# A token shift of 127 partition rows, issued as one transfer or as two of 112 and 15 rows

## The reference

```python
def shift_tokens(t):
    a, s = jnp.split(t, 2, -1)
    s = jnp.pad(s, ((0, 0), (1, 0), (0, 0)))[:, :-1]
    return jnp.concatenate([a, s], -1)

def ffn_layer(x, g, bln, W1, b1, W2, b2):
    mu = x.mean(-1, keepdims=True)
    var = ((x - mu) ** 2).mean(-1, keepdims=True)
    xn = (x - mu) / jnp.sqrt(var + 1e-05) * g + bln
    hg = xn @ W1 + b1
    a, gate = jnp.split(hg, 2, -1)
    return a * jax.nn.gelu(gate, approximate=False) @ W2 + b2

for i in range(DEPTH):                       # 6
    x = attn_layer(shift_tokens(x), Wqkv[i], q_scale[i], k_scale[i], Wo[i]) + x
    x = ffn_layer(shift_tokens(x), ln_g[i], ln_b[i], W1[i], b1[i], W2[i], b2[i]) + x
```

## Time and profile before

| | before |
|---|---|
| median of 3 runs | 1936.04 us |
| the three runs | 1918.3, 1936.04, 7699.03 us |
| the profiled execution's own time | 1925.6 us |
| its span, first to last instruction | 1923.8 us |
| mean granted TensorE clock, share of full speed | 0.928 |

### The profile page before, as it was taken

The page is one execution under the profiler, slowest core; times in us unless marked ns, Lnnn a source line. Parts: engine busy times, 40 slices in busy tenths (PEclk is TensorE's granted clock), DMA queues, the critical chain, the costliest instruction groups (busy, mean ns, idle before and its releaser), DMA issues.

```text
span 1923.8 us, 67850 instructions
## 1 busy us (share of the span) xinstructions
PE 1577.6 (82%) x28560; PEld 1265.7 (66%) x28656; DVE 1382.6 (72%) x2564; ACT 1251.0 (65%) x4601; POOL 1263.7 (66%) x1492
## 2 busy tenths in 40 slices
PE   7588978888879789879789888797898787987974
PEld 5366766766767567667567676676676676766753
DVE  4686876876867778678868777786687686776752
ACT  3376766767757667667667676586676675775761
POOL 2487666776766767667758667676677586776640
PEclk8698989989989999999999899998898998999997
DMA  3011111012111011111111211111211101111110
GB/s 108 13 35 57 39 50 40 26 52 60 35 40 40 27 52 48 43 51 32 40 49 34 60 39 44 30 37 40 60 37 52 41 24 41 42 37 30 36 29 28
DMA packets 50157, 80.61 MB, mean 42 GB/s; under 512 B 8227, under 2 KB 16086, under 8 KB 49854
## 3 DMA queue, kind: packets, MB, share of 16 engines
q1 hardware_dynamic: 49854, 76.27, 14.1%
HBM read 18.62 MB, written 1.05 MB: 10 GB/s over the span
## 4 chain that ended last, share of the span: by engine, by line
PE 46%; DMA 18%; DVE 15%; POOL 9%; ACT 8%; issue 5%; SPq 0%; DVEq 0%; POOLq 0%
DMA xsh<-xr 17%; PE ps L393 6%; PE ps L439 5%; PE ps L449 5%; PE ps L386 5%; ACT pr L647 4%; PE ps L480 4%; PE ps L409 3%; PE ps L388 3%; PE ps L387 3%; DVE t L946 3%; DVE t L948 3%; POOL t L795 3%; PE ps L420 2%; ACT sq L610 2%
## 5 line engine op out<-in xcount | busy, mean ns | idle before, releaser
L776 POOL TENSOR_TENSOR t<-t 128x512 f32<-128x512 f32 x384 | 486.9, 1280 | 86.6 <-DVE t L948 85.4
L647 ACT ACTIVATE pr<-ps,nmax 128x64 f32<-128x64 f32 x1536 | 460.1, 344 | 0.9 <-DVE nmax L963 0.9
L795 POOL TENSOR_TENSOR t<-t,rn 128x512 f32<-128x512 f32 x384 | 397.2, 1056 | 7.5
L393 PE MATMUL ps<-consts,t 128*128 128x128 f32 x1536 | 245.3, 295 | 148.3 <-POOL t L795 138.4
L647 ACT ACTIVATION_READ_ACCUMULATOR pr<-ps,nmax 128x1 f32 x1536 | 364.5, 238 | 0.0
L946 DVE TENSOR_TENSOR t<-ps,rope 128x512 f32<-128x512 f32 x384 | 262.9, 685 | 106.1 <-PE ps L393 74.5
L393 PEld LDWEIGHTS ps<-consts,t 128*128 128x128 f32 x1536 | 192.3, 151 | 204.5 <-POOL t L795 155.8
L610 ACT ACTIVATE sq<-ps 128x512 f32<-128x512 f32 x384 | 230.8, 616 | 107.4 <-PE ps L388 101.1
L386 PE MATMUL ps<-w_hi,xt_hi 128*128 128x512 f32 x576 | 272.2, 473 | 25.6 <-DVE t L948 9.1
L806 POOL TENSOR_TENSOR pr<-pr,rsum 128x512 f32<-128x512 f32 x192 | 201.9, 1052 | 104.0 <-DVE rsum L970 104.0
L948 DVE TENSOR_TENSOR t<-ps,rope 128x512 f32<-128x512 f32 x384 | 261.2, 680 | 0.0
(11 more groups left out here) (122 smaller groups left out, 2732.6 us busy)
## 6 DMA issues: line engine op xcount, KB each, us to landing
v_win<-v SPq DMA_DIRECT2D x384, 128.0 KB, 2.4
wqkv<-wqkv_in SPq DMA_DIRECT2D x36, 256.0 KB, 4.1
xsh<-xr SPq DMA_DIRECT2D x24, 254.0 KB
wo<-wo_in SPq DMA_DIRECT2D x6, 512.0 KB, 14.6
w<-w_in SPq DMA_DIRECT2D x6, 342.0 KB, 4.5
w<-w_in SPq DMA_DIRECT2D x6, 172.5 KB
x<-x_in SPq DMA_DIRECT2D x4, 256.0 KB, 3.9
out<-x SPq DMA_DIRECT2D x4, 256.0 KB, 7.3
```

Source lines behind the costliest of these rows:

```text
L393: i = tr(ps[:, TQ_BANK[c], k * P:(k + 1) * P], t1[:, c, k * P:(k + 1) * P], ident)
L647: i = A(pr[:, c, odd * SPAN:(odd + 1) * SPAN], ps[:, S_BANK[odd], c * SPAN:(c + 1) * SPAN], ACT.Exp, bias=nmax[:, odd, c:c + 1], accum_out ...
L776: G.tensor_tensor(t1[:, c, :], t1[:, c, :], t2[:, c, :], ALU.add).then_inc(qk_added[c], 1)
L795: G.tensor_tensor(w, w, rn[:, par(u), h2, a, :].unsqueeze(2).broadcast_to([P, 8, E]), ALU.mult).then_inc(done, 1)
```

## The change

The transfer of 127 rows becomes two, of rows 0 to 111 and of rows 112 to 126, issued one behind the other and counted on the same semaphore; POOL waits for both. All other instructions of all engines stay what and where they are.

```diff
+SHIFT_PARTS = [(0, 112), (112, 15)]
...
-                sp.dma_start(xsh[1:P, :, :], xr[0:P - 1, s, :]).then_inc(f_shifted, 16)
+                for t, n in SHIFT_PARTS:
+                    sp.dma_start(xsh[t + 1:t + 1 + n, :, :], xr[t:t + n, s, :]).then_inc(f_shifted, 16)
...
             def copy_half(f):
 
                 s = slice(f % NQ * QUAD, f % NQ * QUAD + QUAD)
-                pool.wait_ge(f_shifted, 16 * (f + 1))
+                pool.wait_ge(f_shifted, 16 * len(SHIFT_PARTS) * (f + 1))
                 G.tensor_copy(xsh[:, :, 0:E], xr[:, s, 0:E]).then_inc(f_half, 1)
```

## The result

| | before | after |
|---|---|---|
| median of the runs | 1938.53 us (4 runs) | 1738.72 us (4 runs, 1737.56 to 1739.83) |
| the profiled execution's span | 1923.8 us | 1736.5 us |
| mean granted TensorE clock | 0.928 | 0.967 |

The ratio is 0.900, with a 95% interval of 0.894 to 0.906. One of the four runs before took 7699.03 us and says nothing of the kernel; the ratio leaves it out, the other three are 1918.3, 1936.04 and 1941.03 us. In the later experiments the kernel before took 1925.1, 1927.6 and 1926.3 us (medians of seven). The profiled executions differ by 187.3 us of span; the forecast was 176 us, to 1750.

The account below looks back on a forecast made before the run. No engine is full; the 127-row shift on one DMA engine stalls all four computing engines once in four steps. Waits 136, clock 30 and end 10 sum to 176 us off 1925.6, so 1750 us, range 1730 to 1808.

Parts of the forecast that it names:

- Width of the two parts: Shift transfer: 112 rows spread over the DMA engines, so both parts land in 3.5 us (2.4 to 4.5) instead of 14.08.
- Step 1, POOL: POOL's wait for the shift: POOL is free 5.1 us after the issue, behind the landing, so the transfer leaves the path.
- Step 2, PE and DVE: PE's wait for q at the 23 shifts inside steps: transposes and first rotary come 6.35 us earlier in quad 13; 136 us.
- rival B: DVE becomes the pace: only DVE's own wait is returned and no clock is won; 1807 us, chance 0.12.
- Step 3, the clock: First rotary product to clamp: the clock no longer falls behind PE's pause, 1.3 us a shift on average; 30 us (0 to 40).
- Step 4, the end: Last shift, nothing else left to do: the copy starts 3.5 us after the issue instead of 13.5; 10 us.
- Step 5, SP and `wo`: SP's second issue, about 0.65 us 24 times, costs nothing; `wo` queued behind the shift needs about 7 us, so 0.
- A: The stall goes but the granted clock stays as it is; 1780 us, chance 0.16.
- C: Both parts still go through one DMA engine, the second issue coming on top; 1942 to 1960 us, chance 0.06.
- D: Both parts on one DMA engine, the second starting only when the first has fully landed; 1976 us, chance 0.04.
- The crosscheck by whole steps (1760): Clamp to clamp, stalled step against the one before: 6.8 us times 23 is 156, plus 10 for the end; 1760 us.

Follow-up runs that it names:

- The fills: Kernel before, its one 127-row transfer kept, with 34 or 48 additional identity transposes on PE in the stall: 1915.1 us against 1925.1, and 1901.9 against 1927.6.

## Why the prediction was right

*Width of the two parts.* The mechanism was right. I took 3.5 us for the landing, with 2.4 to 4.5 as bounds; the median was 2.85, but three of the 24 landed outside the bounds, the latest after 5.02 us. The 113-row run shows that the gain hung on the row count of the large part.

*Step 1, POOL.* Right: POOL was free 5.1 us after the issue as before, and never waited inside the steps. With landings of up to 5.02 us that was close. The prediction knows only the rotations as cover; there is a little more, since with 6.5 us nothing shows in the steps either. What I added before the run with 122 and 5 rows, that nearly everything below 10.5 us would be hidden because PE has other work, is wrong too: 8.0 us costs 27 us in the steps. So the cover ends between 6.5 and some 7.5 us here. In all, 6.5 us cost about 6 us, by the trace all of it at the end, and 7.4 and 8.0 about 30.

*Step 2, PE and DVE.* The mechanism was right and the term a little too small, 136 us against 143.4 (138.8 in the second trace of the change). I set the first rotary 1.22 us behind the transposes, the distance read from a step whose clock had fallen. At full clock it is 1065.56 - 1064.64 = 0.92 us; 0.3 us in 23 shifts is 7 us, which is also about what two traces of one kernel differ by. The two engines are ready together, as forecast, and rival B does not occur.

*Step 3, the clock.* 30 us forecast, 31.9 measured. The fills show the cause. I gave the clock the whole 1.7 us of a step that does not split weights; 1.3 us of it is the half clock, and the other 0.35 us is POOL coming late out of its wait, which I had not seen though POOL was busy for 9.32 of the 9.69 us. Over the 18 shifts outside the weight splitting that is about 24 and 6 us; the other five gave only 2 (10.1 to about 9.7 us each), less than the 1.3 each that my average gave them. That the sum came so near is in part luck: the clock was worth less than I said, and POOL's part made up for it.

*Step 4, the end.* 10 us forecast, 11.7 measured:

```profile
1710.75 1.45 SPq L279 DMA_DIRECT2D xsh<-xr  x2
...
1713.65 0.40 POOL L745 COPY xsh<-xr 128x256 f32<-128x256 f32 x1 [11.34 <-DMA xsh<-xr]
```

The copy starts 2.9 us after the issue, not 3.5, which is 10.6 us sooner than before; the last microsecond lies within the 2 us by which this stretch differs between the two traces of the change.

*Step 5, SP and `wo`.* Right that it costs nothing, and `wo` comes sooner than the 7 us that I gave it. The `wo` loads land in

```profile
DMA to landing us min/median/max: 3.7/3.8/6.2
```

(the 6.2 is that of the prologue) against a median of 14.6, and PE waits for none of them.

*Rivals.* A and B fell short of the gain by 41 and 68 us; C and D need both parts on one DMA engine. With 113 and 14 rows the large part is, and even there it was faster than before, since fewer rows stand on the engine. The second part did not wait for the first to land as a whole, as D has it: in the shift of quad 2, 15 of the 17 updates of the transfers' semaphore stand within 5.04 us of the first issue, and only the last two at 12.31 and 12.51 us.

The crosscheck by whole steps (1760) was the worse of the two, since it compared with a step before that was itself 15.4 us long; the changed step took 14.9 with its statistics.

## What to carry to other kernels

Where a transfer in a kernel's path is slow, look at the DMA share while it runs alone: 0.06 is one engine of sixteen. A row count such as 127 or 113, both prime, is worth splitting into a multiple of 16 and a rest. Price a removed stall on each engine that stood still, not by the transfer's length: 11 us less in the transfer gave 7.6 us a shift, and four fifths of that were waits. Do not count on the cover of a later engine: here 1.7 us past POOL's free moment cost nothing in the steps, but 3 us cost 27 us, although PE had hardly to wait.

## What the runs showed of the hardware

- A transfer of 254 KB took 13.9 us as 127 rows and 2.85 us as 112 and 15 (medians); rows of 2048 bytes cost 0.09 to 0.105 us each on an engine that has 41, 61, 113 or 127 of them. The Trainium skill's advice in "DMA: Bandwidth & Descriptors", section "Rules for kernel authors", to use one transfer rather than two for disjoint partition halves, does not hold for such a row count: here the kernel with two took a tenth less time than with one.
- A slow transfer delays others of its queue: `wo`, issued behind the shift, landed in 14.6 us instead of 3.8. In each of these five loads of the trace of before, 15 of the 16 updates of its semaphore stand at 6.6 to 8.0 us after the issue and only the last at 14.3 to 14.8.
- Work without any use made the kernel before faster by 1.3% (0.8 to 1.7%). It filled a pause of 4 to 7.5 us on TensorE, and the granted clock, which had fallen to 1.2 GHz behind this pause in all of the 18 steps without weight splitting, stayed at 2.4 GHz in 16 of them.
